# A mixture-of-experts stage: eight shared tiles run behind the routed ones, rows load while picks are scattered, and TensorE's loop holds eight tiles

## The chip, the cores and the metric

The kernel runs on one core of one Trainium2 chip. The metric is the device time of one execution in microseconds (us), the median of the runs shown. Engines: TensorE (PE, its weight loads PEld), VectorE (DVE), ScalarE (ACT), GpSimd (POOL) and SyncE (SP); SP, ACT and POOL also issue DMAs. A "tile" below is a block of 128 token rows.

## The reference, cut to what matters

Four layers work on x of 4 x 512 tokens with 512 features (2048 tokens, 16 tiles): an attention map, a token-choice block, a cross attention, and last a mixture of experts, the only part that the change touches:

```python
scores = sigmoid(x @ gate_w)                     # 2048 x 32
# two groups of eight experts are ruled out, six experts picked per token
_, selected = top_k(masked_scores, 6)
weights = scores[selected] / sum
g = ragged_dot(xs, w_gate, group_sizes)          # xs: 12288 rows sorted by expert
u = ragged_dot(xs, w_up, group_sizes)            # 512 -> 352
d = ragged_dot(silu(g) * u, w_down, group_sizes) # 352 -> 512
expert_out = sum over the 6 picks of d * weights
shared = silu(x @ sw_gate) * (x @ sw_up) @ sw_down    # width 704
return expert_out + shared                       # added to x
```

All of it is float32. A matmul is made of three passes on values split into a high and a low part.

## The kernel before, in words

The stage is `routed_ffn` (from line 1988 on). Its work for the matrix engine is a row of 159 tiles of one form (`tile`, line 2547): a gate product G (12 matmuls of 352 columns), the turning of the tile before (3 transposes), an up product U (12), and the down product of the tile before (9 matmuls of 512 columns).

- *Shared tiles*, numbers 0 to 31. The shared network of width 704 is done as two halves of width 352, "sets" 0 and 1, on all 16 token tiles each. Their rows are turned by TensorE (`turn_row`, four more transposes), and DVE adds the result to `X` (`add_y`).
- *Routed tiles*, numbers 32 to 158, 127 of them, with set number = expert + 2. Token rows are sorted by expert in the DRAM tensor `d_sorted`. An expert has as many tiles as its rows need, at least one; this data needs fewer than 127, and the tiles left over repeat the last expert. Rows of `d_sorted` are loaded (four 64 KB DMAs and a small one a tile, `load_row`, line 2054; four places are kept), turned by DVE, copied by ACT, and the result `Y` is copied by DVE (`copy_y`, L2336) and stored to `d_y`. The routing weight is picked by DVE (`take_weight`, L2311), for which ACT first copies the wanted experts into a free corner of the G bank (`copy_asked`, L2202). TensorE waits for this (`weighed`).

GpSimd does four things in this order:

- It scatters the token rows into `d_sorted`: 6 picks x 16 token tiles = 96 indirect DMAs (L2149), each of which waits for the one two before (`SCATTERS = 2`).
- It splits the weights of experts 1 to 31 into high and low parts (`split`, L2124 to L2131, and `split_down`). Two buffers are used in turn: expert e's split waits until the up product of expert e-2's last tile is done. Set 2 (expert 0) is split by ACT and DVE during the shared tiles.
- It gathers the results: 96 indirect DMAs that add rows of `d_y` into `X` (L2166), up to four in flight. Pick k of all tokens belongs to experts up to 26 + k, so its 16 gathers wait until those are done. `BETWEEN = 3` gathers follow each of the splits of experts 28, 29 and 30, with a wait for the last of them to land ahead of the next split. The others stand behind the last split.
- SP loads the weights a set ahead, and at the end stores the 16 tiles of `X` as their last gathers land (L2100).

SP's loads of the first four tiles' rows wait until all 96 scatters have landed. The picks of a token are numbered by rising expert, so the first tiles in `d_sorted` hold only rows of low picks: tile j only those of picks 0 to j.

TensorE's routed tiles stand in a loop of two tiles a pass (line 2588). The buffer of a tile's weights is known only at run time: `set_of` (L2545) reads the set's number from the memory into a register, and each tile does so for itself and for the tile before it.

Of the kernel before, what the change touches and what calls it, by code (L numbers as in the profile page):

```python
# [16 lines left out]
P = 128  # L17
# [1318 lines left out]
E_ = 32  # L1336
# [8 lines left out]
TILES = SHARED_TILES + ROUTED_TILES  # L1345
ROW = D + 2 * TOPK
BLOCK = 32
ROWS = 4
SCATTERS = 2
# [638 lines left out]
def routed_ffn(nc, c):  # L1988
# [6 lines left out]
    with ExitStack() as stack:  # L1995
# [9 lines left out]
        row = [hs[:, n, 0:D] for n in range(ROWS)]  # L2005
        side = [hs[:, n, D:ROW] for n in range(ROWS)]
# [30 lines left out]
            nc, c, "e_", "y_even y_odd asked_copied weight_taken x_stored set_high")  # L2037
        y_stored = [y_even, y_odd]
# [5 lines left out]
            nc, c, "e_", "midT_high_ready midT_low_ready down_done y_copied")  # L2044
        sorted_tiles = c.dram["d_sorted"].rearrange("(t p) d -> p t d", p=P)
# [8 lines left out]
        QUAD_END = (TILES - 1 - ROWS) // ROWS  # L2054

# [10 lines left out]
        def _(sp):  # L2066
# [30 lines left out]
            for t in range(NT):  # L2097

                sp.wait_ge(gathered[t % GATHERS], 16 * ((NT * (TOPK - 1) + t) // GATHERS + 1))
                sp.dma_start(c.out.rearrange("b (j p) d -> p (b j) d", p=P)[:, t, :], c.X[:, t, :]).then_inc(x_stored, 16)  # L2100
# [3 lines left out]
        def _(pool):  # L2104
# [48 lines left out]
            split(3, 1, 0, SHARED_TILES)  # L2153
            def expert_done(e):
                return pool.value_load(tiles_through[0:1, e:e + 1], min_val=1, max_val=TILES)

            def gather(numbers):
                for n in numbers:
                    k, t = divmod(n, NT)
                    if t == 0:  # L2160

                        arrived(y_copied, pool.value_load(tiles_through[0:1, E_ + k:E_ + k + 1], min_val=SHARED_TILES, max_val=TILES + 2))
# [8 lines left out]
            with pool.Fori(2, E_ // 2 - 1) as n:  # L2171
                for par in range(2):
                    done = pool.value_load(tiles_through[0:1, bass.ds(n * 2 + (par - 4), 1)], min_val=1, max_val=TILES)
# [16 lines left out]
        def _(act):  # L2190
            def load(i, place):

                act.wait_ge(weight_taken, i - SHARED_TILES + 1)
                act.wait_ge(blocks_turned, i - SHARED_TILES + 1)
                load_row(act, bass.ds(i + ROWS - SHARED_TILES, 1), place)

            def copy_asked(i, par, place, loads, taken=None):

                act.wait_ge(row_loaded[place], LANDED * loads)
                if taken is not None:  # L2200
                    act.wait_ge(weight_taken, taken)
# [6 lines left out]
            def copy_rowT(i, par):  # L2208
                act.wait_ge(row_turned, i + 1)
                nc.scalar.copy(rowT_high[par][:], XT.rearrange("p (k n) -> p k n", k=CC)).then_inc(rowT_high_ready, 1)  # L2210

            def copy_blocks(i, par):
                act.wait_ge(blocks_turned, i - SHARED_TILES + 1)
# [10 lines left out]
            def store(i, par):  # L2224
                act.wait_ge(y_copied, i + 1)
                act.dma_start(y_tiles[:, bass.ds(i - SHARED_TILES, 1), :], y[par][:].unsqueeze(1)).then_inc(y_stored[par], 16)
# [8 lines left out]
            def routed_steps(i, place, fills, loads=True, stores=True, more=True):  # L2235
                par = place % 2
                if more:
                    copy_blocks(i + 1, 1 - par)
                    copy_asked(i + 1, 1 - par, (place + 1) % ROWS, fills, i - SHARED_TILES if stores else None)
# [28 lines left out]
            for i in range(NT + 2, SHARED_TILES - 1):  # L2268
                steps(i, i % 2)
            steps(SHARED_TILES - 1, 1, more=False)  # L2270
            copy_blocks(SHARED_TILES, 0)
# [409 lines left out]
```

## Time and profile before

| | us |
|---|---|
| runs | 2270.92 (median), 2274.73, 2268.97 |
| profiled execution | 2273.54 |
| its span, first to last instruction | 2271.7 |
| TensorE busy in the span | 1927.4 (85%) |
| GpSimd busy | 1004.5 (44%) |
| VectorE busy | 1251.2 (55%) |
| ScalarE busy | 581.7 (26%) |

The profile is of one execution. Busy time is an average over four layers; the stage in question runs from about 1128 us to the end. An operation's line is that of the kernel shown above. "Idle before" is the time for which an engine stood still ahead of an instruction, and the releaser is what ended it; "issue" means that no wait shown in the profile explains it. The 40 slices of the page show TensorE at nine tenths or more over most of this stage, and nearly idle in the last slice, while GpSimd is at eight tenths and the DMA engines at nine.

### The profile page before, as it was taken

How to read it: one execution, taken by the hardware profiler on the slowest of the kernel's cores; microseconds unless marked ns; L12 is line 12 of the kernel's file. 1: busy time of each engine (PE TensorE's matmuls, PEld its weight loads, DVE VectorE, ACT ScalarE, POOL GpSimd, SP SyncE). 2: the span in 40 equal slices, each digit the busy share in tenths (PEclk: the TensorE clock that was granted, in tenths of full speed). 3: DMA queues.
4: the chain of work that ended last, by engine and by line, in shares of the span. 5: the costliest groups of instructions: out<-in, count | busy, mean ns of one | idle time of the engine just before them, and what ended most of it. 6: DMA issues, size and time to landing. Idle time of an engine off the chain costs nothing.

```text
span 2271.7 us, 34535 instructions
## 1 busy us (share of the span) xinstructions
PE 1927.4 (85%) x10056; PEld 1388.2 (61%) x10057; DVE 1251.2 (55%) x2357; ACT 581.7 (26%) x1291; POOL 1004.5 (44%) x552
## 2 busy tenths in 40 slices
PE   5956887877887489998799999999999999998991
PEld 3423443653333133333389988888888888887881
DVE  2555443556776757775674435555555555554550
ACT  3320222501114244453222212222222222221220
POOL 0000000002547355655025555556555757757886
PEclk9987998898996789999899999999999999999996
DMA  3033100503124457621124445556555656656999
GB/s 117 0 103 116 46 28 19 185 2 104 74 93 147 147 195 243 206 95 33 33 91 176 181 154 164 156 154 190 161 156 154 192 158 191 183 155 159 208 205 212
DMA packets 272642, 306.03 MB, mean 135 GB/s; under 512 B 40857, under 2 KB 184217, under 8 KB 272569
## 3 DMA queue, kind: packets, MB, share of 16 engines
q1 hardware_dynamic: 144216, 187.78, 25.7%
q10 hardware_dynamic: 106848, 66.34, 10.7%
q0 software_dynamic: 21504, 50.93, 9.5%
q8 instruction: 46, 0.75, 0.1%
q14 instruction: 28, 0.22, 0.0%
HBM read 186.42 MB, written 118.55 MB: 134 GB/s over the span
## 4 chain that ended last, share of the span: by engine, by line
PE 37%; POOL 7%; issue 3%; DMA 2%; DVE 1%; POOLq 0%; ACT 0%; DVEq 0%
PE psum L2515 15%; PE psum L2535 8%; PE psum L2520 7%; POOL X L2166 6%; PE psum L2540 4%; PE psum L2509 2%; DMA X<-d_y,f_slots 2%; PE psum L2502 1%; POOL e_gu_low L2131 0%; POOL e_d_low L2115 0%; DVE e_gu_low L2350 0%; POOL e_gu_high L2126 0%; POOL e_d_low L2116 0%; DVE e_d_low L2350 0%; DVE f_arena L2377 0%
## 5 line engine op out<-in xcount | busy, mean ns | idle before, releaser
L2515 PE MATMUL psum<-e_gu_high,e_rowT_high 128*128 (+1 forms) x1272 | 432.1, 341 | 52.2 <-issue 40.6
L2515 PE MATMUL psum<-e_gu_low,e_rowT_high 128*128 (+1 forms) x1272 | 410.7, 325 | 0.0
L2515 PEld LDWEIGHTS psum<-e_gu_high,e_rowT_high 128*128 128x128 f32 x1272 | 241.6, 190 | 87.4 <-issue 83.9
L2520 PE MATMUL psum<-e_gu_high,e_rowT_low 128*128 (+1 forms) x1272 | 257.6, 325 | 0.0
L2515 PEld LDWEIGHTS psum<-e_gu_low,e_rowT_high 128*128 128x128 f32 x1272 | 242.4, 191 | 3.7
L2216 ACT CAST e_rowT_high<-psum 128x512 fp32r<-128x512 f32 x127 | 74.5, 587 | 643.4 <-DVE psum L2297 602.3
L2520 PEld LDWEIGHTS psum<-e_gu_high,e_rowT_low 128*128 128x128 f32 x1272 | 214.8, 190 | 0.0
L2336 DVE COPY f_arena<-psum 128x512 f32<-128x512 f32 x127 | 87.9, 692 | 191.7 <-PE psum L2540 187.2
L2535 PE MATMUL psum<-e_d_high,e_midT_high 128*128 (+3 forms) x477 | 188.4, 395 | 1.0 <-ACT e_midT_high L2222 1.0
L2535 PE MATMUL psum<-e_d_low,e_midT_high 128*128 (+3 forms) x477 | 187.6, 393 | 0.0
L2124 POOL CAST e_gu_high<-f_gu_in 128x1408 fp32r<-128x1408 f32 x31 | 42.1, 1358 | 281.4 <-PE psum L2520 258.3
L2166 POOL DMA_INDIRECT X<-d_y,f_slots x96 | 149.4, 1556 | 38.3 <-issue 25.5
L2149 POOL DMA_INDIRECT d_sorted<-f_hs,f_slots x96 | 97.1, 1012 | 116.4 <-DMA d_sorted<-f_hs,f_slots 70.9
L2297 DVE STREAM_TRANSPOSE psum<-f_hs 128x512 f32<-128x512 f32 x127 | 139.6, 1099 | 0.0
L2540 PE MATMUL psum<-e_d_high,e_midT_low 128*128 (+3 forms) x477 | 137.0, 395 | 0.7 <-DVE e_midT_low L2318 0.6
L2302 DVE TENSOR_TENSOR e_rowT_low<-psum,e_rowT_high 128x512 fp32r<-128x512 f32 x127 | 87.8, 692 | 82.9 <-ACT e_rowT_high L2216 77.0
L2206 ACT ACTIVATE e_silu<-psum 128x352 f32<-128x352 f32 x159 | 74.1, 466 | 195.6 <-PE psum L2520 164.5
L1152 POOL TENSOR_TENSOR x_hrstd<-x_hrstd,minus_half 128x64 f32<-128x64 f32 x7 | 79.8, 11394 | 94.9 <-DVE x_hrstd L1178 94.9
L2316 DVE TENSOR_TENSOR e_midT_low<-psum,e_midT_high 128x256 fp32r<-128x256 f32 x159 | 67.5, 424 | 89.9 <-ACT e_midT_high L2222 80.1
L2328 DVE SCALAR_TENSOR_TENSOR e_mid<-e_silu,e_row_weight,psum 128x352 f32<-128x352 f32 x127 | 73.8, 581 | 78.2 <-issue 53.0
L548 POOL TENSOR_TENSOR b_r_ms<-b_r_ms,minus_half 128x2 f32<-128x2 f32 x2 | 1.4, 695 | 248.9 <-DVE b_r_ms L540 248.9
L1042 PE MATMUL psum<-y_k_high,y_q_high 32*128 32x512 f32 x256 | 66.8, 523 | 49.3 <-DVE f_hs L1052 26.6
(382 smaller groups left out, 3856.7 us busy)
## 6 DMA issues: line engine op xcount, KB each, us to landing
d_sorted<-f_hs SPq DMA_DIRECT2D x32, 1048.0 KB, 10.2
d_y<-f_arena ACTq DMA_DIRECT2D x127, 256.0 KB
f_hs<-d_sorted ACTq DMA_DIRECT2D x492, 64.0 KB
f_gu_in<-in_L_ffn_w_gate SPq DMA_DIRECT2D x32, 704.0 KB
f_gu_in<-in_L_ffn_w_up SPq DMA_DIRECT2D x32, 704.0 KB
f_d_in<-in_L_ffn_w_down SPq DMA_DIRECT2D x32, 512.0 KB
d_y<-f_hs SPq DMA_DIRECT2D x8, 1024.0 KB, 5.7
f_d_in<-in_L_ffn_w_down SPq DMA_DIRECT2D x32, 192.0 KB
```

Source lines behind the costliest of these rows:

```text
L1152: nc.gpsimd.tensor_tensor(hrstd[:, a, :], hrstd[:, a, :], c.minus_half[:, 0:JT * H], ALU.pow).then_inc(hrstd_ready, 1)
L2149: nc.gpsimd.indirect_dma_start(c.dram["d_sorted"], bass.IndirectOffsetOnAxis(ap=slots[:, k, t:t + 1], axis=0), hs[:, t, :], None).then_inc ...
L2166: nc.gpsimd.indirect_dma_start(c.X[:, t, :], None, c.dram["d_y"], bass.IndirectOffsetOnAxis(ap=slots[:, k, t:t + 1], axis=0), compute_op=A ...
L2206: nc.scalar.activation(silu[par][:], G[par][:, 0:M], ACT.Silu).then_inc(silu_ready, 1)
L2216: nc.scalar.copy(rowT_high[par][:].rearrange("p k (n b) -> p k n b", b=BLOCK), XT.rearrange("p (n k b) -> p k n b", k=CC, b=BLOCK)).then_i ...
L2297: nc.vector.transpose(XT.rearrange("p (n k b) -> p n k b", k=CC, b=BLOCK), row[place].rearrange("p (n b k) -> p n k b", k=CC, b=BLOCK)).th ...
L2302: nc.vector.tensor_tensor(rowT_low[par][:].rearrange("p k (n b) -> p k n b", b=BLOCK), XT.rearrange("p (n k b) -> p k n b", k=CC, b=BLOCK) ...
L2336: nc.vector.tensor_copy(y[par][:], Y[par]).then_inc(y_copied, 1)
L2515: nc.tensor.matmul(bank[:, 0:M].unsqueeze(1), rowT_high[par][:, k, :], w[:, bass.ds(buffer, 1), k, at:at + M], start=(k == 0 and n == 0), ...
L2520: last = nc.tensor.matmul(bank[:, 0:M].unsqueeze(1), rowT_low[par][:, k, :], gu_high[:, bass.ds(buffer, 1), k, at:at + M], start=False, st ...
L2535: nc.tensor.matmul(Y[par].unsqueeze(1), midT_high[0:n, k, :], w[0:n, bass.ds(buffer, 1), k, :], start=(k == 0 and m == 0), stop=False)
L2540: last = nc.tensor.matmul(Y[par].unsqueeze(1), midT_low[0:n, k, :], d_high[0:n, bass.ds(buffer, 1), k, :], start=False, stop=(k == ME - 1))
```

## The change

The constants are `LATE = 8`, `R0 = 24` (the first routed tile), `R1 = 151` (the first late tile) and a new set, `LATE_SET = 34`, which is shared set 1 loaded once more. Shared set 1 on token tiles 8 to 15 now runs behind the routed tiles. Since `X` is being gathered into at that time, the late results are held in `hs` (`hold_y`) and added to `X` at the end, when that token tile's last gather has landed; the gathers take token tiles 8 to 15 first. GpSimd splits one set more and does one more group of three gathers ahead of it. Scatters are four in flight. SP loads the rows of tiles 0 to 5 as soon as picks 0 to j have landed; the places of the rows are moved to another area, so that `hs` stays whole. The wanted experts are copied into the U bank instead of G, TensorE no longer waits for the picking, and DVE picks the weight ahead of the low part. TensorE's loop has eight tiles a pass, each tile's set number is read once, ahead of the down product, and handed on. Places where only tile numbers are written anew are left out.

```diff
+LATE = 8
+R0 = SHARED_TILES - LATE
+R1 = R0 + ROUTED_TILES
+LATE_SET = E_ + 2
-SCATTERS = 2
+SCATTERS = 4
...
-        row = [hs[:, n, 0:D] for n in range(ROWS)]
-        side = [hs[:, n, D:ROW] for n in range(ROWS)]
+        row = [c.hot_flat[:, (n + 1) * D:(n + 2) * D] for n in range(ROWS)]
...
-        ASKED = [G[n][:, M:M + TOPK] for n in range(2)]
+        ASKED = [U[n][:, M:M + TOPK] for n in range(2)]
...
-        LOOP_END = (TILES - 3) // 2
+        PE_LOOP = 8
+        LOOP_END = (R1 - 1) // PE_LOOP
...
-            for landed in scattered:
-                sp.wait_ge(landed, NT * TOPK // SCATTERS * 16)
-            sp.wait_ge(row_turned, NT + ROWS)
-            for n in range(ROWS):
-                load_row(sp, slice(n, n + 1), n)
+            sp.wait_ge(slots_ready, TOPK)
+            for j in range(TOPK):
+
+                for landed in scattered:
+                    sp.wait_ge(landed, NT * (j + 1) // SCATTERS * 16)
+                if j >= ROWS:
+                    sp.wait_ge(weight_taken, j - ROWS + 1)
+                    sp.wait_ge(blocks_turned, j - ROWS + 1)
+                load_row(sp, slice(j, j + 1), j % ROWS)
             with sp.Fori(2, E_) as e:
                 expert(e)
...
+            half = slice(M, 2 * M)
+            load(LATE_SET, "(k p) n -> p k n", c.dram["L1_ffn_sw_gate"][:, half], c.dram["L1_ffn_sw_up"][:, half], c.dram["L1_ffn_sw_down"][half, :])
+            for m in range(NT):
+                t = (m - LATE) % NT
+
+                if m < LATE:
+                    sp.wait_ge(late_added, m + 1)
+                else:
+                    sp.wait_ge(gathered[m % GATHERS], 16 * (gathered_last(m) // GATHERS + 1))
...
             for e in range(E_ - 4, E_):
                 split(e + 2, e % 2, e - 1, expert_done(e - 2))
-                if e < E_ - 1:
-                    last = gather(range(BETWEEN * (e - E_ + 4), BETWEEN * (e - E_ + 5)))
-                    pool.wait_ge(gathered[last % GATHERS], 16 * (last // GATHERS + 1))
-            gather(range(BETWEEN * 3, NT * TOPK))
+                last = gather(range(BETWEEN * (e - E_ + 4), BETWEEN * (e - E_ + 5)))
+                pool.wait_ge(gathered[last % GATHERS], 16 * (last // GATHERS + 1))
+            split(LATE_SET, LATE_SET % 2, LATE_SET - 3, expert_done(E_ - 2))
+            gather(range(BETWEEN * 4, NT * TOPK))
...
+            def hold_y(i, par):
+
+                dve.wait_ge(down_done, i + 1)
+                if i < R1 + 2:
+                    dve.wait_ge(y_stored[par], 16 * ((i - 2 - R0) // 2 + 1))
+                nc.vector.tensor_copy(hs[:, token_of(i), 0:D], Y[par]).then_inc(y_copied, 1)
...
                     turn_blocks(i + 1, (place + 1) % ROWS, fills)
+                    take_weight(i + 1, 1 - par, (place + 1) % ROWS)
                     low_blocks(i + 1, 1 - par)
-                    take_weight(i + 1, 1 - par, (place + 1) % ROWS)
...
+            dve.wait_ge(y_copied, TILES)
+            for m in range(LATE):
+                dve.wait_ge(gathered[m % GATHERS], 16 * (gathered_last(m) // GATHERS + 1))
+                x = c.X[:, NT - LATE + m, :]
+                nc.vector.tensor_tensor(x, x, hs[:, NT - LATE + m, 0:D], ALU.add).then_inc(late_added, 1)
...
-                if weighed is not None:
-                    pe.wait_ge(weight_taken, weighed)
                 pe.wait_ge(rowT_high_ready, i + 1)
...
                 product(U[par], par, buffer, M).then_inc(up_done, 1)
                 if also is not None:
                     pe.wait_ge(also, 1)
+                following = set_of(ahead) if ahead is not None else None
                 if old is not None:
                     down(i - 1, 1 - par, old, before)
+                return following
...
-            with pe.Fori(SHARED_TILES // 2 + 1, LOOP_END) as n:
-                tile(n * 2, 0, set_of(n * 2), set_of(n * 2 - 1), used=n * 2 - 1, before=n * 2 - 2,
-                     weighed=n * 2 - SHARED_TILES + 1)
-                tile(n * 2 + 1, 1, set_of(n * 2 + 1), set_of(n * 2), used=n * 2, before=n * 2 - 1,
-                     weighed=n * 2 + 2 - SHARED_TILES)
...
+            def routed_tiles(first, many, old, turns=None):
+
+                e = set_of(first)
+                for q in range(many):
+                    following = tile(first + q, q % 2, e, old, used=first + (q - 1), before=first + (q - 2),
+                                     turns=(turns if q + 1 == many else None), ahead=(first + (q + 1) if q + 1 < many else None))
+                    e, old = following, e
+                return old
+
+            routed_tiles(R0, PE_LOOP, 1)
+            with pe.Fori(R0 // PE_LOOP + 1, LOOP_END) as n:
+                routed_tiles(n * PE_LOOP, PE_LOOP, set_of(n * PE_LOOP - 1))
+            last = routed_tiles(LOOP_END * PE_LOOP, R1 - LOOP_END * PE_LOOP, set_of(LOOP_END * PE_LOOP - 1), turns=R1)
+            for i in range(R1, TILES):
+                tile(i, i % 2, LATE_SET, last if i == R1 else LATE_SET, turns=(i + 1 if i + 1 < TILES else None),
+                     used=i - 1, before=i - 2)
```

## Rows read from the trace of the kernel before

**Rows 1.** The page's part 4: the chain that ended last, by engine.
```profile
PE 37%; POOL 7%; issue 3%; DMA 2%; DVE 1%; POOLq 0%; ACT 0%; DVEq 0%
```

**Rows 2.** The chain in order of time from 2020 us: start, us, step.
```profile
2023.03 1.64 POOL X L2166
2026.83 5.98 DMA X<-d_y,f_slots
...
2073.33 1.56 POOL X L2166
...
2099.32 1.59 POOL X L2166
...
2119.83 7.42 DMA X<-d_y,f_slots
```

**Rows 3.** GpSimd's timeline: start, us, instruction, idle before and releaser.
```profile
2084.93 1.36 POOL L2124 CAST e_gu_high<-f_gu_in 128x1408 fp32r<-128x1408 f32 x1 [6.32 <-DMA X<-d_y,f_slots]
...
2087.55 3.20 POOL L2128 TENSOR_TENSOR e_gu_low<-f_gu_in,e_gu_high 128x1408 fp32r<-128x1408 f32 x1
...
2260.18 1.55 POOL L2166 DMA_INDIRECT X<-d_y,f_slots  x1 [0.65 <-DMA X<-d_y,f_slots]
```

**Rows 4.** Stretches: us, busy (x instructions) by engine, clock, DMA share, GB/s.
```profile
1500.00:1600.00 100.00, 95.40 (x540) 86.51 (x539) 55.90 (x120) 22.57 (x75) 56.45 (x33) 1.00 0.56 165
...
2140.00:2216.00 76.00, 69.46 (x382) 61.16 (x381) 38.53 (x82) 15.35 (x50) 63.27 (x42) 1.00 1.06 206
2216.00:2272.00 56.00, 7.38 (x38) 5.91 (x37) 3.20 (x7) 1.42 (x5) 38.06 (x25) 0.59 0.98 213
```

**Rows 5.** ScalarE's timeline: the silu of shared tiles 23 and 31.
```profile
1291.45 0.46 ACT L2206 ACTIVATE e_silu<-psum 128x352 f32<-128x352 f32 x1 [5.30 <-PE psum L2520]
...
1345.17 0.46 ACT L2206 ACTIVATE e_silu<-psum 128x352 f32<-128x352 f32 x1 [5.41 <-PE psum L2520]
```

**Rows 6.** ScalarE's and TensorE's timelines at the first routed tile.
```profile
1351.23 0.59 ACT L2216 CAST e_rowT_high<-psum 128x512 fp32r<-128x512 f32 x1 [5.17 <-DVE psum L2297]
...
1353.09 0.65 PE L2515 MATMUL psum<-e_gu_high,e_rowT_high 128*128 x1 [3.63 <-DVE e_picked L2311]
```

**Rows 7.** TensorE's timeline: the first matmul of single tiles, the last of them tile 158.
```profile
1534.71 0.32 PE L2515 MATMUL psum<-e_gu_high,e_rowT_high 128*128 x1
...
1541.63 0.42 PE L2515 MATMUL psum<-e_gu_high,e_rowT_high 128*128 x1 [0.50 <-issue]
...
1548.05 0.32 PE L2515 MATMUL psum<-e_gu_high,e_rowT_high 128*128 x1
...
1555.16 0.43 PE L2515 MATMUL psum<-e_gu_high,e_rowT_high 128*128 x1 [0.68 <-issue]
...
2021.76 0.43 PE L2515 MATMUL psum<-e_gu_high,e_rowT_high 128*128 x1 [0.46 <-issue]
...
2214.14 0.43 PE L2515 MATMUL psum<-e_gu_high,e_rowT_high 128*128 x1 [0.74 <-issue]
```

**Rows 8.** GpSimd: the scatters of line 2149, and two splits.
```profile
L2149 POOL DMA_INDIRECT d_sorted<-f_hs,f_slots x96: 963/968/2290, 1166.2 to 1340.7; - x96
...
1224.52 0.97 POOL L2149 DMA_INDIRECT d_sorted<-f_hs,f_slots  x1 [0.79 <-DMA d_sorted<-f_hs,f_slots]
...
1227.59 0.97 POOL L2149 DMA_INDIRECT d_sorted<-f_hs,f_slots  x1 [0.82 <-DMA d_sorted<-f_hs,f_slots]
...
1347.54 1.36 POOL L2124 CAST e_gu_high<-f_gu_in 128x1408 fp32r<-128x1408 f32 x1 [5.92 <-issue]
...
1378.43 1.36 POOL L2124 CAST e_gu_high<-f_gu_in 128x1408 fp32r<-128x1408 f32 x1 [11.91 <-PE psum L2520]
```

**Rows 9.** DMA queues, TensorE's instructions: the whole span, then 271 to 308 us.
```profile
q8 instruction: 46, 0.75, 0.1%
...
q8 instruction: 1, 0.02, 0.2%
```

More of the change, by code:

```diff
@@ L2044, in routed_ffn, with token_of, turned, gathered_last @@
             nc, c, "e_", "midT_high_ready midT_low_ready down_done y_copied")
+        def token_of(i):
+            return NT - LATE + i - R1 if i >= R1 else i % NT
+        def turned(i):
+            return R0 + i - R1 + 1 if i >= R1 else i + 1
+        def gathered_last(m):
+            return NT * (TOPK - 1) + m
         sorted_tiles = c.dram["d_sorted"].rearrange("(t p) d -> p t d", p=P)
@@ L2191, in load, with copy_asked @@
             def load(i, place):
[L2193 to L2197, printed above, removed]
+                act.wait_ge(weight_taken, i - R0 + 1)
+                act.wait_ge(blocks_turned, i - R0 + 1)
+                load_row(act, bass.ds(i + ROWS - R0, 1), place)
+            def copy_asked(par, place, loads):
                 act.wait_ge(row_loaded[place], LANDED * loads)
[L2200 to L2201 removed]
                 nc.scalar.copy(ASKED[par], side[place][:, TOPK:2 * TOPK]).then_inc(asked_copied, 1)
@@ L2238, in routed_steps @@
                     copy_blocks(i + 1, 1 - par)
-                    copy_asked(i + 1, 1 - par, (place + 1) % ROWS, fills, i - SHARED_TILES if stores else None)
+                    copy_asked(1 - par, (place + 1) % ROWS, fills)
                 silus(i, par)
@@ L2470, in _ @@
-            with dve.Fori(SHARED_TILES // ROWS + 1, QUAD_END) as n:
-                for q in range(ROWS):
-                    routed_steps(n * ROWS + q, q, n + ((q + 1) // ROWS + 1 - SHARED_TILES // ROWS))
-                    copy_y(n * ROWS + q - 1, 1 - q % 2, 16 * (n * 2 + (q - 1) // 2 - SHARED_TILES // 2))
-            for i in range(QUAD_END * ROWS, TILES):
-                routed_steps(i, i % ROWS, (i + 1 - SHARED_TILES) // ROWS + 1, more=(i + 1 < TILES))
-                copy_y(i - 1, (i - 1) % 2, 16 * ((i - 1 - SHARED_TILES) // 2))
@@ L2477, in _ @@
-            low_midT(TILES - 1)
-            copy_y(TILES - 1, (TILES - 1) % 2, 16 * ((TILES - 1 - SHARED_TILES) // 2))
-            for i in (TILES - 1, TILES - 2):
-                dve.wait_ge(y_stored[i % 2], 16 * ((i - SHARED_TILES) // 2 + 1))
-                dve.nop().then_inc(y_copied, 1)
+            turn_blocks(R0, 0, 1)
+            take_weight(R0, 0, 0)
+            low_blocks(R0, 0)
+            routed_steps(R0, 0, 1)
+            add_y(R0 - 1, 1)
+            for i in range(R0 + 1, R0 + ROWS):
+                routed_steps(i, i % ROWS, (i + 1 - R0) // ROWS + 1)
+                copy_y(i - 1, (i - 1) % 2, 16 if i == R0 + 3 else None)
@@ new lines, in _ @@
+            with dve.Fori(R0 // ROWS + 1, QUAD_END) as n:
+                for q in range(ROWS):
+                    routed_steps(n * ROWS + q, q, n + ((q + 1) // ROWS + 1 - R0 // ROWS))
+                    copy_y(n * ROWS + q - 1, 1 - q % 2, 16 * (n * 2 + (q - 1) // 2 - R0 // 2))
+            for i in range(QUAD_END * ROWS, R1):
+                routed_steps(i, i % ROWS, (i + 1 - R0) // ROWS + 1, more=(i + 1 < R1))
+                if i + 1 == R1:
+                    low_rowT(R1, R1 % 2)
+                copy_y(i - 1, (i - 1) % 2, 16 * ((i - 1 - R0) // 2))
@@ new lines, in _ @@
+            for i in range(R1, TILES):
+                low_midT(i - 1)
+                if i + 1 < TILES:
+                    low_rowT(i + 1, (i + 1) % 2)
+                multiply(i, i % 2)
+                if i == R1:
+                    copy_y(R1 - 1, (R1 - 1) % 2, 16 * ((R1 - 1 - R0) // 2))
+                else:
+                    hold_y(i - 1, (i - 1) % 2)
+            low_midT(TILES - 1)
+            hold_y(TILES - 1, (TILES - 1) % 2)
+            dve.wait_ge(y_copied, TILES)
[3 more added lines that the diff above has]
+                nc.vector.tensor_tensor(x, x, hs[:, NT - LATE + m, 0:D], ALU.add).then_inc(late_added, 1)
@@ L2544, in set_of, with tile @@
             def set_of(i):
-                return pe.value_load(tile_set[0:1, bass.ds(i - SHARED_TILES, 1)], min_val=2, max_val=E_ + 1)
-            def tile(i, par, e, old, turns=False, used=None, before=None, also=None, weighed=None):
-                if weighed is not None:
-                    pe.wait_ge(weight_taken, weighed)
+                return pe.value_load(tile_set[0:1, bass.ds(i - R0, 1)], min_val=2, max_val=E_ + 1)
+            def tile(i, par, e, old, turns=None, used=None, before=None, also=None, ahead=None):
                 pe.wait_ge(rowT_high_ready, i + 1)
```

91 lines of the change are left out of this document (41 added, 50 removed).

## The prediction, made before the changed kernel ran

> **What bounds the kernel now.** I read the page's chain first, then the chain of waits in order of time from 2000 us on, then GpSimd's timeline there, then the stretches, and last the places that the diff touches.
>
> The page gives TensorE 37% of the chain, GpSimd 7% and DMA 2% [rows 1]. In order of time the chain runs on TensorE until 2008 and then changes engine: from the first gather at 2023.03 it stays on GpSimd and its transfers until the end [rows 2]. The reader is to see three things there. Between two groups of three gathers lies a wait for the landing (5.98 us) and the split of one expert's weights, so that a group comes every 25 to 26 us (2073.33 to 2099.32) [rows 2]. From 2099.32 on, 87 gathers follow one another, the last at 2260.18, that is 160.86 us for 86 steps, 1.87 us each [rows 2, 3]. And the span ends 11.5 us behind the start of the last one (its landing and the last store of the output). TensorE begins its last tile at 2214.14 [rows 7] and has 7.38 us of work in the last 56 us [rows 4]. So the end is set by GpSimd: the moment of its first gather, plus what it issues behind it. That first gather waits for a result of the matrix engine, the output of the tiles up to expert 26; ahead of 2023 every microsecond of TensorE counts, and behind it TensorE only fills in.
>
> **Part 1, eight shared tiles moved behind.** Ahead of the routed tiles go eight tiles' time: the silu of tile 23 starts at 1291.45, that of tile 31 at 1345.17 [rows 5], 53.7 us. All of it stands ahead of the first gather, so: -53.7.
>
> The moved tiles cost TensorE the same again, but at the end. Do they set it? GpSimd's events keep their distance to the first gather. The last expert's gate weights are split 67.7 us behind it (2087.55 + 3.20 less 2023.03) [rows 2, 3]; with the first gather at 1946.8 (below) that is 2014.5. Then 18 routed tiles at the pace that they have under the gathers (a routed tile is 24 + 3 + 9 = 36 matmuls; 382 in 76 us make 7.16 us a tile, against 6.67 for the 540 in 100 us of the quiet stretch) [rows 4], 129 us, eight shared ones, 54 us, and what follows the start of a last tile, about 3 us more than a tile: 2200. One copy and eight additions of 0.7 us make it 2207. The last gather lands about 2212. TensorE is not late, by 5 us; if its tiles run faster than now, by more. The eight late tiles load no rows and store none, so the gathers have less beside them.
>
> **Part 2, the turn from shared to routed tiles.** TensorE stood idle 3.63 us ahead of the first routed tile, until the weight was picked (1353.09), while the turned rows had been copied by 1351.82 (1351.23 + 0.59) [rows 6]. The new code waits for that copy and no longer for the picking: -1.0. That rows load earlier brings nothing here: the copy followed the vector engine's own work, not a landing. Bounds: 0 and -1.3.
>
> **Part 3, eight tiles in one body of TensorE's loop.** A tile inside the body takes 6.42 us (1541.63 to 1548.05). A tile that ends at the loop's edge takes 6.92 (from 1534.71) and 7.11 (from 1548.05), with 0.50 and 0.68 us idle "issue" behind [rows 7]. So an edge costs 0.60 on the mean. From the first routed tile (1353.09) to tile 132 (2021.76), the one at whose start the first gather is let go, lie 100 tiles [rows 6, 7] with 50 edges; in the new loop 12.5 remain. 37.5 x 0.60 = 22.5. Against it: the number of the next tile's weight buffer is now read ahead of the second product, on the path of its addresses. The trace has no row for such a read. Today two of them lie inside the body without a gap, and two and the branch cost 0.60 at an edge; so one costs between 0 and 0.30 a tile. I take 0 for most of the tiles, and charge 1 us in all: -21.5. The bounds are +4 (0.30 on 87 inner tiles against 22.5) and -24.
>
> **Part 4, a fifth weight set for GpSimd.** One more group of three gathers is followed by a landing wait, and one more split (the late shared set) is put in. Price: a period of the chain, 25.99 (2073.33 to 2099.32) [rows 2], but three gathers leave the stream, 3 x 1.87 = 5.6: +20.4 on the path, all of it, since GpSimd waits for nothing else there. Its loads go out on SP's queue behind the last expert's and have some 60 us for what takes 20 elsewhere. Bounds: +14 (the split alone, no landing wait) and +23.
>
> **Part 5, four scatters in flight, rows loaded as they are scattered.** 96 scatters ran from 1166.2 to 1340.7, a median of 0.97 us each and mostly a wait for the one two before [rows 8]: the one started at 1224.52 let the one at 1227.59 go, so it took 3.07 us. Four in flight leave 3.07/4 = 0.77, less than the 0.97 + 0.30 that issuing takes: 96 x 1.27 = 122 us, plus some 10 for the loads beside them, end about 1298. This is worth nothing by itself but is needed: GpSimd must split expert 1 behind its scatters. It did so at 1347.54 [rows 8], long ahead of its use, and expert 0 has four tiles (its buffer was free at 1378.43 [rows 8]). With everything 54.7 earlier, expert 1's first tile comes at about 1326, and its gate needs the split begun by 1320 (5.8 us from the first cast to the end of the low part [rows 3]). 1298 suffices by 22. Cost 0; bounds 0 and +27 (scatters as slow as now). SP's six row loads stand ahead of expert 2's weights, which wait for expert 1's split anyway: 0. The pick of the weight ahead of the low part on the vector engine: 0.2 to 0.3 us, under the 3 us that the next product leaves it: 0.
>
> **Sum.** -53.7 - 1.0 - 21.5 + 20.4 = -55.8. Against the profiled execution, 2273.54 us around a span of 2271.7: span 2215.9, time 2217.7. The median shown, 2270.92, lies 2.6 below that execution; in its terms 2215.
>
> **A rule against the change.** TensorE's earlier loop (line 750) makes two passes, 271 to 308 us and 309 to 347. In the first, one packet came on its instruction queue q8 [rows 9]; behind the jump back, in the second, that queue has none. So the block that it had left was still there. On going back three blocks nothing is shown. 46 blocks carry 0.75 MB [rows 9], 16 KB each. The Trainium skill, "Runtime: NRT & Kernel Launch", "Instruction fetch mechanics", says that the instruction memory is two cache lines and that a taken branch outside the current two pages stalls for a fetch; it also gives TensorE 2048 instructions. By the first figure each back edge of an eight-tile body would miss, by the second none; the loop in the trace speaks for more than two.
>
> **Rivals.** *Refetch at the back edge.* The body has at least 8 x 72 = 576 matmul and weight-load instructions (540 + 539 in 15 tiles [rows 4]) against 144 now, several blocks instead of about one. For: the quiet loop may owe its lack of fetches to its two tiles. Against: the kept block above. At 0.8 us for a block (0.1% of 16 engines' span over 46 [rows 9]) up to about 2 with its latency, 12 edges ahead of the first gather: +10 to +24, 2225 to 2239. Chance 0.11. *The edge moves inside.* The read ahead of the second product costs 0.2 to 0.3 a tile: the loop brings little; 2215 + 20 = 2235. Chance 0.09. *Scatters stay slow* (DMA bound, not bound by two in flight): expert 1 late by up to 27: 2242. Chance 0.07. *Slower than before: the gather stream.* A gather lands 7.42 us behind its start [rows 2], and four in flight at 1.87 make 7.5, so every rise in latency becomes pace. The DMA engines show 1.06 at 2140 to 2216 and 0.98 behind [rows 4]. 83 steps lie in the stream; from 55.8/83 = 0.67 more a step, 2.54 us, the change is a loss; at 2.8 it is 2292. Against: the pace held at 1.87 in both stretches, with and without row loads. Chance 0.04. *The moved tiles don't cover it* (TensorE ends last): at 7.5 us a tile +5, 2220; inside the forecast's own range.
>
> **Numbers.** Forecast 2215, own range 2200 to 2227 (the bounds of parts 2, 4 and small faults of 3), chance 0.67; 0.02 for a sum of mishaps near no change. To leave out no more than 2 in 10 with the 27 us of the scatters and the 24 of the fetch: 2199 to 2243. A time within 0.3% (6.8 us) counts as no change. Faster 0.94, same 0.02, slower 0.04.
>
> **What would show it.** Steps 1 and 2: the first routed tile at about 1298, with some 2.6 us idle. Step 3: tile starts 6.4 apart, a gap every eighth; instruction blocks in the loop's time mean the first rival. Step 4: first gather at 1947, four groups 25 to 26 apart, then 84 gathers at 1.87, the last at 2204. Step 5: last scatter before 1310. It would be wrong if the first gather came behind 1965 or the gathers went slower than 1.95.

## The result, and the profile after

The changed kernel takes 2201.89 us (median of 4 runs, 2200.39 to 2203.55) beside 2271.49 for the kernel before (median of 4, 2268.97 to 2274.73): ratio 0.9693, 95% interval 0.9676 to 0.971, so faster by 3.1%, 69.6 us. Forecast were 2215, inside 2199 to 2243; the time stands near the low edge. On another chip (the last experiment below) the ratio was 0.9703 (0.9688 to 0.9718).

The profiled execution took 2200.39 us around a span of 2198.6, at a mean granted clock of 0.932, 73.1 us less than the one of before. Not all of that belongs to the change: the expert stage, counted from TensorE's first product, begins earlier. TensorE's timeline of before and of after, at that product:

```profile
1131.11 0.63 PE L2515 MATMUL psum<-e_gu_high,e_rowT_high 128*128 128x352 f32 x1 [2.59 <-DVE e_gu_low L2350]
```
```profile
1123.04 0.63 PE L2563 MATMUL psum<-e_gu_high,e_rowT_high 128*128 128x352 f32 x1 [2.59 <-DVE e_gu_low L2386]
```

8.07 us of the difference lie ahead of anything that the diff touches; the stage itself went from 1140.6 us (2271.7 - 1131.1) to 1075.6 (2198.6 - 1123.0), 65 us. In what follows times are taken from that first product, "stage" for short.

**The end of the stage.** The page's chain by engine, against [rows 1], and the chain in order of time from the first gather on, against [rows 2]:

```profile
PE 35%; POOL 7%; DMA 3%; issue 2%; DVE 1%; POOLq 0%; ACT 0%; DVEq 0%
...
1927.22 1.64 POOL X L2194
...
1931.02 6.16 DMA X<-d_y,f_slots
...
1939.23 1.36 POOL e_gu_high L2153
...
1952.36 1.56 POOL X L2194
...
1977.62 1.56 POOL X L2194
...
2003.69 1.59 POOL X L2194
...
2029.91 1.57 POOL X L2194
```

Four groups now, where there were three. Each has a landing wait (6.16 us in the first) and a split; the groups and the stream behind them start 25.1 to 26.2 us apart. GpSimd's timeline, against [rows 3], and TensorE's at the first tile of the gathers and at the last tile of all, against [rows 7]:

```profile
2186.48 1.55 POOL L2194 DMA_INDIRECT X<-d_y,f_slots  x1 [0.30 <-DMA X<-d_y,f_slots]
```
```profile
1925.33 0.33 PE L2563 MATMUL psum<-e_gu_high,e_rowT_high 128*128 x1
...
2158.62 0.32 PE L2563 MATMUL psum<-e_gu_high,e_rowT_high 128*128 128x352 f32 x1
```

The stream of 84 gathers runs from 2029.91 to 2186.48, 83 steps of 1.886 us, and the span ends 12.1 us behind the start of the last. From the first gather to the end there are 271.4 us, where there were 248.7: +22.7. TensorE begins its last tile at 2158.62, 28 us ahead of the last gather.

**Where the stage's time went.** The stretches, against [rows 4] (us, then busy time and count of PE, PEld, DVE, ACT, POOL, the clock, the DMA share, GB/s):

```profile
1500.00:1600.00 100.00, 99.86 (x571) 92.56 (x570) 58.12 (x127) 23.37 (x80) 62.27 (x35) 1.00 0.61 171
2029.00:2105.00 76.00, 75.97 (x436) 70.60 (x435) 44.06 (x96) 17.53 (x60) 63.08 (x42) 1.00 1.04 209
...
2168.00:2198.00 30.00, 0.32 (x2) 0.00 (x0) 5.82 (x9) 0.00 (x0) 16.52 (x10) 0.54 0.97 243
```

At 36 matmuls a tile the quiet stretch now gives 100 x 36/571 = 6.30 us a tile, against 6.67, and the stretch under the gathers 76 x 36/436 = 6.28, against 7.16. The waits of TensorE from 1400 to 1900 us say the same from the other side (what waited, what for: us in all, times, longest); before it is this row, after the view is empty there:

```profile
PE psum L2515 <- issue: 20.4, 37, 0.7
```

TensorE's single tile starts, against [rows 7], the second pair around the end of one eight-tile body:

```profile
1501.83 0.32 PE L2563 MATMUL psum<-e_gu_high,e_rowT_high 128*128 x1
...
1508.10 0.33 PE L2563 MATMUL psum<-e_gu_high,e_rowT_high 128*128 x1
...
1539.53 0.32 PE L2563 MATMUL psum<-e_gu_high,e_rowT_high 128*128 x1
1546.05 0.43 PE L2563 MATMUL psum<-e_gu_high,e_rowT_high 128*128 x1
```

6.27 us inside the body, 6.52 at its edge (from 1539.53). The turn to the routed tiles, against [rows 5, 6] (ScalarE, then TensorE), and the scatters with the split behind them, against [rows 8]:

```profile
1283.43 0.46 ACT L2232 ACTIVATE e_silu<-psum 128x352 f32<-128x352 f32 x1 [5.30 <-PE psum L2568]
...
1290.47 0.66 PE L2563 MATMUL psum<-e_gu_high,e_rowT_high 128*128 x1 [2.75 <-ACT e_rowT_high L2242]
```
```profile
L2176 POOL DMA_INDIRECT d_sorted<-f_hs,f_slots x96: 963/969/2187, 1158.1 to 1292.0; - x96
...
1292.92 1.37 POOL L2151 CAST e_gu_high<-f_gu_in 128x1408 fp32r<-128x1408 f32 x1
```

The account of the stage, each a difference of two starts in TensorE's or GpSimd's timeline:

| stretch | before | after | change | forecast |
|---|---|---|---|---|
| first product to first routed tile | 222.0 | 167.4 | -54.6 | -54.7 |
| 100 routed tiles from there | 668.7 | 634.9 | -33.8 | -21.5 |
| from there (the start of the 101st) to the first gather | 1.3 | 1.9 | +0.6 | 0 |
| first gather to the end | 248.7 | 271.4 | +22.7 | +20.4 |
| stage | 1140.6 | 1075.6 | -65.0 | -55.8 |

### The profile page after: what moved, and what is told of

Its sections match the earlier page's. It is cut to its first block and busy times, and to the rows that moved or that the text cites. A ratio compares the mean times of both kernels' runs of the same rounds, so it can differ in the third digit from the quotient of the medians.

```text
span 2198.6 us, 33697 instructions
## 1 busy us (share of the span) xinstructions
PE 1903.9 (87%) x10056; PEld 1391.0 (63%) x10057; DVE 1248.0 (57%) x2365; ACT 576.2 (26%) x1291; POOL 1019.9 (46%) x560
## 5 line engine op out<-in xcount | busy, mean ns | idle before, releaser
L2563 PE MATMUL psum<-e_gu_high,e_rowT_high 128*128 (+1 forms) x1272 | 427.4, 337 | 17.9 <-POOL e_gu_low L2155 10.9
L2326 DVE STREAM_TRANSPOSE psum<-f_arena 128x512 f32<-128x512 f32 x127 | 139.5, 1098 | 0.0
L1042 PE MATMUL psum<-y_k_high,y_q_high 32*128 32x512 f32 x256 | 66.1, 517 | 49.7 <-DVE f_hs L1052 27.1
L2588 PEld LDWEIGHTS psum<-e_d_high,e_midT_low 128*128 128x128 f32 (+1 forms) x477 | 89.7, 188 | 22.7 <-DVE e_midT_low L2347 1.6
L2155 POOL TENSOR_TENSOR e_gu_low<-f_gu_in,e_gu_high 128x1408 fp32r<-128x1408 f32 x32 | 103.4, 3231 | 0.0
L2158 POOL TENSOR_TENSOR e_gu_low<-f_gu_in,e_gu_high 128x1408 fp32r<-128x1408 f32 x32 | 103.0, 3219 | 0.0
```

The lines of the kernel that those rows point to most:

```text
L2155: nc.gpsimd.tensor_tensor(gu_low[:, par, :, 0:M], gu_in[:, :, 0:M], gu_high[:, par, :, 0:M].bitcast(F32), ALU.subtract).then_inc(gate_spli ...
L2158: nc.gpsimd.tensor_tensor(gu_low[:, par, :, M:2 * M], gu_in[:, :, M:2 * M], gu_high[:, par, :, M:2 * M].bitcast(F32), ALU.subtract).then_i ...
L2326: nc.vector.transpose(XT.rearrange("p (n k b) -> p n k b", k=CC, b=BLOCK), row[place].rearrange("p (n b k) -> p n k b", k=CC, b=BLOCK)).th ...
L2563: nc.tensor.matmul(bank[:, 0:M].unsqueeze(1), rowT_high[par][:, k, :], w[:, bass.ds(buffer, 1), k, at:at + M], start=(k == 0 and n == 0), ...
L2588: last = nc.tensor.matmul(Y[par].unsqueeze(1), midT_low[0:n, k, :], d_high[0:n, bass.ds(buffer, 1), k, :], start=False, stop=(k == ME - 1))
```

## Experiments

Theory: the end is the first gather plus GpSimd's chain; the first gather moves with every microsecond that TensorE gains ahead of it; the loop gained 34 us, partly by its length and partly because one set is read a tile where two were. Rivals for each term are in the expectations. "Stage" is measured as above, against the changed kernel's 1075.6. Experiments 1 to 10 are one run each, on other chips than the result's. How far such figures repeat can be seen where the code is the same: the stage of the changed kernel was 1075.6 and 1073.9, that of experiment 7 was 1050.3 and 1053.3, and the 100 routed tiles took 632.6 to 634.9 us in the six profiles whose code leaves those tiles as they are (the changed kernel twice, experiments 5, 7, 9 and 11). A difference of 3 us between two stages is therefore not read as an effect.

**1. A two-tile loop, the set still handed on.**

```diff
-        PE_LOOP = 8
+        PE_LOOP = 2
```

> The changed kernel with two tiles a pass of TensorE's loop instead of eight; the set number is still read once a tile, ahead of the down product, and handed on. Changed kernel: 2202 us, inner tiles 6.27 us, edges 6.51 to 6.57 plus 0.1 behind, so about 0.35 an edge. Theory 1 (an edge costs what the changed kernel's edges cost, 0.35, since the number's read is what made it dear before): 37.5 more edges ahead of the first gather, +13 us, 2215, pairs of 12.9 us. Theory 2 (an edge of a two-tile loop costs 0.60 as before, the branch and its restart are the price): +22, 2224, pairs of 13.15. If the loop length were worth nothing: 2202.

2218.93 us; stage 1091.1, +15.6; the 100 tiles took 651.5 (+16.6). Its stretch and its waits on "issue" from 1400 to 1900:

```profile
1500.00:1600.00 100.00, 98.29 (x552) 89.08 (x551) 56.46 (x124) 22.08 (x75) 58.98 (x34) 1.00 0.61 173
...
PE psum L2563 <- issue: 5.9, 19, 0.4
```

The time lies between those of the two theories. Where one set is read a tile, the length of the body is worth 16.6 us of 100 tiles, and the read the other 17.2 (668.7 in the kernel before less 651.5): 552 matmuls, between 540 and 571. Of the two-tile loop's idle "issue" (20.4 us in before) most is gone although the loop has as many edges. So those gaps came from the second read more than from the branch (the stretches of experiment 2 show it for all 100 tiles).

**2. The eight-tile loop with two sets read at the start of each tile, as before.**

```diff
-                following = set_of(ahead) if ahead is not None else None
...
-                e = set_of(first)
...
+                    e = set_of(first + q)
+                    if q > 0:
+                        old = set_of(first + (q - 1))
```

> The changed kernel, eight tiles a pass, but each tile reads its own set number and the one before at its start, as the kernel before did. Theory 1 (the inner tile fell from 6.42 to 6.27 because one read instead of two stands in the way): inner tiles 6.35 to 6.42 again, +0.1 x 87 = +9 to +13 us, 2211 to 2215. Theory 2 (inner tiles were hidden anyway and only the edges went): +0 to +2, 2202 to 2204.

2208.64 us; stage 1083.2, +7.7; the 100 tiles 643.3, +8.4: theory 1, a little under its figure. A tile inside the body took 6.28 to 6.49 us, mostly 6.4. A single read handed on is worth 8.4 us of 100 tiles in this loop, 0.08 a tile. In the two-tile loop it was worth twice that (17.2, experiment 1). And the loop's length is worth 25.4 with two reads (668.7 less 643.3). The terms overlap. The same 100 tiles as stretches, in the kernel before, experiment 1, experiment 2 and the changed kernel, then TensorE under the gathers in experiment 2:

```profile
1353.09:2021.76 668.67, 641.16 (x3600) 582.61 (x3601) 373.20 (x800) 150.15 (x500) 393.27 (x222) 1.00 0.58 169
```
```profile
1293.50:1944.99 651.49, 641.20 (x3601) 582.78 (x3601) 368.22 (x800) 147.63 (x500) 400.07 (x226) 1.00 0.62 175
```
```profile
1289.89:1933.15 643.26, 640.35 (x3601) 581.66 (x3601) 367.84 (x800) 146.80 (x500) 400.53 (x226) 1.00 0.63 177
...
2036.00:2112.00 76.00, 73.93 (x411) 66.10 (x411) 42.34 (x90) 16.44 (x56) 63.00 (x42) 1.00 1.05 207
```
```profile
1290.47:1925.33 634.86, 633.72 (x3601) 588.01 (x3601) 367.12 (x800) 146.30 (x500) 400.52 (x226) 1.00 0.64 179
```

TensorE stood idle 27.5 us in the kernel before, 10.3 with the single read in the short loop, 2.9 with two reads in the long one, 1.1 in the changed kernel. In the short loop the second read costs idle time alone, 17.2 us, with the busy time the same (641.2). In the long loop 6.6 of its 8.4 us lie in the busy time.

**3. Two scatters in flight.**

```diff
-SCATTERS = 4
+SCATTERS = 2
```

> The changed kernel with two scatters in flight instead of four. Theory 1 (the prediction's part 5): the scatters take 175 us as before and end at 1333 instead of 1292; expert 1's split starts behind them, its gate's low part is ready at 1340, 21 us later than its first tile began (1318), and the whole chain behind moves by that: 2202 + 21 = 2223. Rival (the split of expert 1 has slack that the later experts' waits give back, since GpSimd idles 4 to 12 us an expert there): below +10, 2202 to 2212.

2225.5 us, stage 1101.2, +25.6. The scatters (duration min/median/max, first and last start) and what GpSimd waited for ahead of them, then TensorE at expert 1's first tile:

```profile
L2176 POOL DMA_INDIRECT d_sorted<-f_hs,f_slots x96: 965/971/2146, 1157.6 to 1334.4; - x96
...
  DMA d_sorted<-f_hs,f_slots: 75.6, 81
```
```profile
1341.35 0.66 PE L2563 MATMUL psum<-e_gu_high,e_rowT_high 128*128 x1 [20.10 <-POOL e_gu_low L2155]
```

Theory 1 holds. Part 5 brings nothing by itself and 26 us of part 1 hang on it: GpSimd splits expert 1 behind its scatters. The other half of part 5, the early row loads, is kept here: the first routed tile begins at 1289.87 while scatters go out until 1334.4. What it would cost to load the rows behind all scatters again, no run shows.

**4. A 24-tile loop.**

```diff
-        PE_LOOP = 8
+        PE_LOOP = 24
```

> The changed kernel with 24 tiles a pass of TensorE's loop, at least 24 x 72 = 1728 matmul and weight-load instructions and with register work some 2500. Theory 1 (about 2048 instructions stay): the passes fetch their blocks anew, some 10 packets a pass on q8, 30 to 40 more than the 52 of the changed kernel less what the straight parts add, and each back edge costs 1 to 3 us: 2202 - 4 + 4 x 2 = 2203 to 2210. Theory 2 (more stays, or sequential fetching hides it): no packets in the loop's time, 4 edges fewer: 2199.

2216.14 us, stage 1091.4, +15.9; the 100 tiles 649.6, +14.7. In the changed kernel q8, the queue of TensorE's instructions, has no packet from 1400 to 2070; here it has the first row below from 1400 to 1900. The second row is TensorE at a back edge, the two after it the last tile of the body and the first of the next:

```profile
q8 instruction: 34, 0.56, 0.5%
```
```profile
1755.46 0.66 PE L2563 MATMUL psum<-e_gu_high,e_rowT_high 128*128 x1 [3.80 <-issue]
```
```profile
1745.20:1755.50 10.30, 6.50 (x38) 5.71 (x36) 6.20 (x13) 2.11 (x7) 10.22 (x6) 0.92 0.56 161
1755.50:1764.20 8.70, 8.70 (x36) 8.27 (x37) 1.20 (x3) 1.00 (x3) 2.29 (x2) 0.70 0.61 186
```

This is the forecast's first rival, a refetch on going back, at a body three times as long. Its price was taken too low, here too (2203 to 2210 were expected): an edge costs 10.3 + 8.7 - 2 x 6.3 = 6.4 us, of which 3.8 are the idle time that the row shows and 2.4 the next tile at a granted clock of 0.70. Three such edges lie in the 100 tiles, 19 us, less some 4 for the twelve short edges that are gone. The packets come all through a pass, some ten in each, so the whole body is fetched anew; away from the jump most tiles take 6.24 to 6.33 us, as without packets. The eight-tile body, with 8 x 72 = 576 matmul and weight-load instructions, is kept whole; that of 24, with 1728 and the waits and address operations beside them, is not. The Trainium skill, "Runtime: NRT & Kernel Launch", "Instruction fetch mechanics", gives TensorE 2048 instructions and says that the instruction memory is two cache lines. The first figure agrees with both kernels, if the waits and register operations bring the 24-tile body above it, which no count here shows; the second would have had the eight-tile body refetched, and q8 shows none.

**5. Four shared tiles behind.**

```diff
-LATE = 8
+LATE = 4
...
+            at = R0 % PE_LOOP
-                routed_tiles(n * PE_LOOP, PE_LOOP, set_of(n * PE_LOOP - 1))
+                routed_tiles(n * PE_LOOP + at, PE_LOOP, set_of(n * PE_LOOP + at - 1))
```

> LATE = 4: four of the shared tiles run behind the routed tiles, twelve ahead. Theory 1 (what the number of late tiles is worth is the time of those tiles ahead of the first routed tile, and the end is set by the stream of gathers that starts a fixed number of tiles later): the first gather comes 4 x 6.7 = 26.8 us later than in the changed kernel, the stream keeps its length, span 2198.6 + 27 = 2226, time 2229. Theory 2 (part of the gain of eight came from the tail, where TensorE's slack is limited, or the first routed tile then no longer waits): 2210 to 2220.

2226.22 us, stage 1099.8, +24.2. GpSimd's first gather:

```profile
1953.59 1.64 POOL L2194 DMA_INDIRECT X<-d_y,f_slots  x1 [8.16 <-DVE f_arena L2365]
```

It comes 24.8 us later in the stage (829.0, 804.2 in the changed kernel), and first gather to end keeps its length (270.8). The four tiles cost 27.1 ahead of the first routed tile (194.5 against 167.4), and 100 routed tiles were 2.3 shorter. Theory 1 within 3 us.

**6. Twelve shared tiles behind.** The edit is that of experiment 5, with 12.

> LATE = 12: twelve of the shared tiles run behind, four ahead. Theory 1 (the gain goes on until something else ends last): the first gather could come 26.8 us earlier, but expert 1's gate is split about 7.5 us after it would be wanted, and TensorE with twelve tiles behind the routed ones now ends close to the gathers' end; 2202 - 19 = 2183, 2188 if the late sums bind too. Theory 2 (only the gathers' stream counts): 2175. Theory 3 (the end is already TensorE's, or the late sums take as much as is gained): 2198 to 2206.

2196.08 us, stage 1069.1, -6.5, where theory 1 gave -14 to -19 and theory 3 -4 to +4. GpSimd did gain 20.6 (last gather at 1042.8 of the stage, 1063.4 in the changed kernel). But from 1990 us on the whole chain is TensorE's, and its end reads:

```profile
2179.10 0.71 PE psum L2588 x3
...
2179.83 0.70 DVE f_hs L2380
...
2180.55 0.69 DVE X L2530
...
2181.85 6.01 DVE X L2530 x10
```

TensorE's last product is followed by the copy and the additions of the late tiles. It had lost time on both sides of the routed tiles: 6.26 us at the first one (the turned rows were not there) and 3.19 at the next expert's, and in the same two places under the gathers as the changed kernel. So the rival "TensorE ends last" is real, from somewhere between eight and twelve tiles.

**7. No landing wait ahead of the four splits.**

```diff
                 last = gather(range(BETWEEN * (e - E_ + 4), BETWEEN * (e - E_ + 5)))
-                pool.wait_ge(gathered[last % GATHERS], 16 * (last // GATHERS + 1))
```

> GpSimd no longer waits, ahead of the splits of its last four sets, for the landing of the gathers that it has just issued. Theory 1 (each of the four waits is idle time in GpSimd's chain of splits and gathers, which sets the end): 4 x 5.5 us = 22 us less, 2180. Theory 2 (the transfers then run beside the split and slow it, or TensorE's sets come late for another reason): the time is given back, 2195 to 2205.

2177.31 us, stage 1050.3, -25.3. What GpSimd's splits waited for from 1924 us to the end, in the changed kernel:

```profile
POOL e_gu_high L2151 <- DMA X<-d_y,f_slots: 23.9, 4, 6.5
```

Here that row is gone, and by the profile, whose spans on GpSimd are rough, a split begins in the tail of the third gather:

```profile
1931.17 1.54 POOL L2194 DMA_INDIRECT X<-d_y,f_slots  x1 [0.30 <-issue]
1932.14 1.94 POOL L2151 CAST e_gu_high<-f_gu_in 128x1408 fp32r<-128x1408 f32 x1
...
1934.77 3.81 POOL L2155 TENSOR_TENSOR e_gu_low<-f_gu_in,e_gu_high 128x1408 fp32r<-128x1408 f32 x1
...
1947.14 1.56 POOL L2194 DMA_INDIRECT X<-d_y,f_slots  x1
```

The low parts take 3.81 beside landing gathers, against 3.2 [rows 3], so a little is given back, but the period falls from 25.7 to 19.8 (12 gathers in 79.0 against 102.7). The weights also come in time: TensorE's waits of 5.25 and 5.62 us for a split, at 1969.28 and 1995.34 in the changed kernel, are gone. Theory 1 holds, 3 us better than its figure, which is no more than the spread. By the code the waits are needed by nothing behind them: the split reads and writes weights alone, and each gather still waits for the one four before it.

**8. The kernel before with the loop alone.**

```diff
-            with pe.Fori(SHARED_TILES // 2 + 1, LOOP_END) as n:
...
+            routed_tiles(SHARED_TILES, PE_LOOP, 1)
+            with pe.Fori(SHARED_TILES // PE_LOOP + 1, LOOP_END) as n:
+                routed_tiles(n * PE_LOOP, PE_LOOP, set_of(n * PE_LOOP - 1))
```

> The kernel before with one edit of the change alone: the routed tiles on TensorE run in an eight-tile loop that hands the next tile's set on, where they ran in a two-tile loop that read two sets a tile. Theory 1 (the loop is worth 0.34 us a tile, and the gathers' stream moves with the first hundred routed tiles): 2271 - 34 = 2237 (2232 beside a run of 2266). Theory 2 (before, the two-tile loop's idle time lay beside other waits, weight_taken among them, which this kernel keeps): 2245 to 2260.

2234.49 us, 30.4 under the 2264.93 of the kernel before on the same chip; stage 1106.0, -34.6 against the 1140.6 of before. 100 tiles took 634.0, 34.7 less. So the loop brings 30 us by two single times and 35 by the stage, without any other part of the change, and TensorE's wait for the picked weight, which this kernel keeps, costs nothing in these tiles.

**9. Eight gathers in flight,** on top of experiment 7.

```diff
-GATHERS = 4
+GATHERS = 8
```

> GATHERS = 8 on top of the kernel without the four landing waits (2177 in its run): eight gathers may be in flight where four were. Theory 1 (the stream's step of 1.86 us is GpSimd's own, 1.55 busy and 0.30 between, and no gather waits for the one four before it): 2177, within 3. Theory 2 (the landing of the gather four before sets the step): the step falls to 1.6 and the stream of 84 gains up to 20 us, until TensorE ends last about 7 us earlier: 2170.

2179.97 us, stage 1052.0. The gathers, and all that GpSimd waited for ahead of them:

```profile
L2194 POOL DMA_INDIRECT X<-d_y,f_slots x96: 1539/1555/2103, 1930.2 to 2164.5; - x96
...
  issue: 27.9, 93
  DVE f_arena L2364: 8.5, 2
```

No gather waits for another's landing any more, and 96 of them take 234.3 us as in experiment 7 (234.0). The step of 1.86 is GpSimd's own, 1.55 and 0.30; the second and third gather of all take the same 1.55 at 1929 to 1933 us in the changed kernel, where the DMA share was 0.55 (1926 to 1933).

**10. The pick of the weight behind the low part,** with the wait on TensorE that this order needs.

```diff
+                    low_blocks(i + 1, 1 - par)
                     take_weight(i + 1, 1 - par, (place + 1) % ROWS)
-                    low_blocks(i + 1, 1 - par)
...
+                if weighed is not None:
+                    pe.wait_ge(weight_taken, weighed)
```

> The changed kernel with VectorE's pick of the weight behind the low part of the row again, and with TensorE's wait for it ahead of the tile that this order needs. Theory 1 (the order was free to choose: both are done well ahead of their readers, and only tile 25, whose low part came late, moves): 2202 less 0 to 2. Theory 2 (TensorE's extra wait against a register costs its sequencer time at each of 127 tiles, as the reads of sets did): 2204 to 2210.

2201.1 us, stage 1076.6: no difference. The first routed tile came 1.0 later in the stage (168.4), the one behind it 0.5 sooner after that, and 100 tiles took 635.7 (+0.8).

**11. Experiment 7 once more, timed.** The same edit.

> The kernel without the four landing waits once more, timed. If the first run of it (2177, 24 to 25 us under the changed kernel) holds: ratio to the kernel before 0.961 (2177 over 2265), and 0.989 to the changed kernel. If that run was a good one by chance: 2183 to 2200.

2178.56 us (median of 5, 2176.66 to 2181.5), ratio to the kernel before 0.9601 (0.9588 to 0.9614): the gain holds, and this version beats both kernels.

**12. The changed kernel once more,** on the chip of experiment 11 and with the same runs of before (2267.77, median of 9).

> The changed kernel once more, on this chip. Theory 1 (the 8 us that its profile had gained ahead of the stage that the change touches are the spread of single executions, and only 65 belong to the change): ratio 0.971 to 0.972, some 65 us under the kernel before. Theory 2 (something ahead of the stage became faster with the change): ratio 0.968 to 0.969, 70 to 73 us under.

2201.32 us (median of 4), ratio 0.9703 (0.9688 to 0.9718), 66.5 us under the kernel before, between the two theories. Its own profile has the stage begin at 1126.68 and last 1073.9; the twelve other profiles of the changed kernel and of the experiments begin it between 1122.5 and 1126.7, among them experiment 8, whose code ahead of the stage is that of before. So 1131.11 was most likely a late one and the 8 us mostly the spread of executions; the kernel before was profiled only once. An effect of 1 or 2 us there is not excluded.

## Why the prediction was right, and where its sum was off

**What bounds the kernel: right.** Experiments 3, 5, 7 and 8 each moved the first gather or GpSimd's chain behind it, and the end moved by the same amount within 3 us.

**Part 1: right.** With part 2, -54.6 against -54.7. That TensorE's moved tiles are covered was right too, but by more than was forecast: a cover of 5 us at 7.16 us a tile under the gathers. The pace there is now 6.28. With the second read back it is 76 x 36/411 = 6.66 (experiment 2), and with one read in the short loop 74 x 36/402 = 6.63 (experiment 1, from 2050 us on). So the gathers slow a tile only where a second read or the short loop stands in it as well, and TensorE ends about 30 us ahead of the span. The forecast had only "if its tiles run faster than now, by more" for this: that it was covered was foreseen, the width of the cover was not. Experiment 6 shows how far the cover goes.

**Part 2: right.** Idle 2.75 where 2.6 was forecast, waiting for the copy, not the pick.

**Part 3: the term that was mis-sized,** by 12 us, and most of the distance between 2215 and 2202. For the handed-on read only a cost was looked for: "I take 0 for most of the tiles, and charge 1 us in all". In fact the change takes one of two reads away, and that brings 8.4 us in the eight-tile loop (experiment 2): 9.4 of the 12.3. "A tile inside the body takes 6.42 us" was held constant. That is so with two reads, where most take 6.4, and not with one, where they take 6.27. The length alone, with two reads as before, brings 25.4 where 22.5 were forecast, the other 2.9, and so passes the bound of -24 by itself; the prediction gives no working for that bound. Taken in the other order, the read brings 17.2 in the short loop and the length then 16.6 (experiment 1). By the stretches of experiment 2, 26.4 of the 33.8 us are idle time that is gone, and 7.4 lie inside the busy time, where no idle row shows them. What the matmuls wait for there is not shown; that it is their addresses is a guess.

**Part 4: right to 2.3 us.** The fourth period made the groups 26.4 us longer (102.7 against 76.3; 25.99 was taken), the stream lost only 4.3 of the 5.6 us of its three gathers, as its step is 1.886 and not 1.87, and the end came 0.6 later behind the last gather. Experiment 7 shows that of the whole term some 6 us are the landing wait, and 24 with the three older ones.

**Part 5: right.** The last scatter starts 133.9 us behind the first (132 forecast: 122 and 10 for the loads), with a median step of 1.27 and a mean of 1.41; without it 26 us are lost (27 forecast). The order of the pick cost 0 (experiment 10).

**The rivals.** Refetch at the edge: did not occur at eight tiles, does at 24. (The earlier loop fetched one block in its first pass, so it could not speak for more than two blocks, as the prediction had it; the eight-tile body does.) The edge moved inside: no, the inner tile became shorter. Slow scatters: no. The gather stream: the forecast's "every rise in latency becomes pace" was too strong. 11 gathers waited for a landing, 4.5 us in all; with eight in flight none does and the pace stays. TensorE ends last: only with twelve late tiles.

**The remainder.** The forecast's -55.8, with 12.3 more gained in part 3, 2.3 lost in part 4 and 0.6 lost ahead of the first gather, makes the stage's -65.0 but for rounding; what the medians show beyond it, 69.6 on the first chip and 66.5 on the second, lies in the unexplained spread ahead of the stage. That part is chance, and on the first chip it brought the time some 5 us closer to the range's low edge.

## What to carry to other kernels

A short loop on TensorE with addresses out of registers pays for each value it reads, for the most part in small idle gaps and in part inside the busy time: compare matmuls per 100 us with and without, and hand values on rather than reading them twice. Lengthen the body, but watch the instruction queue: eight tiles were kept, 24 were fetched anew, and where between them the limit lies was not tried. When the end is one engine's chain, look in it for waits that nothing behind them needs: here four landing waits, one of them added by the change, were worth 24 us, a third of what the whole change brought. Work moved behind a chain is free only as long as the engine that gets it has slack; eight tiles were covered, twelve were not.

## What the runs showed of the hardware

- A back edge of TensorE's 24-tile body cost 6.4 us: 3.8 idle, and a next tile of 8.7 us at a granted clock of 0.70, where others take 6.3. The edges of the eight-tile body cost some 0.35, with no packet on q8: 0.25 in the tile at the edge (6.52 against 6.27) and 0.1 in the one behind it (6.38 on the mean).
- A second read of a set costs 0.17 us a tile in a two-tile body, all of it idle time (27.5 us of 100 tiles against 10.3), and 0.08 in an eight-tile one, most of it inside the busy time (640.4 against 633.7). Beside the gathers it costs more, 0.38 (6.66 against 6.28).
- Scatters go at a median of 1.27 us with four in flight (0.97 busy, 0.30 between), 1.41 on the mean, gathers with addition at a median of 1.86 with four or eight: there GpSimd is the limit, at a DMA share of 0.97 to 1.04 in the stretches shown.
- By the profile's rough spans a split on GpSimd begins before the instruction of the last gather has ended (1932.14 against 1931.17 + 1.54). It is slower beside landing gathers, 3.81 against 3.2 us for a low part; the sum was still 6 us a group shorter than with the wait.
